# A four-layer graph network on one core: one square, one gate, 24 pieces and 100 products moved

## The reference, cut to what matters

```python
z = xx @ W_fc.T
e = sigmoid(concat([z[src], z[dst]]) @ W_attn.T)
w = exp(e - segment_max(e, dst)[dst])
h = segment_sum(w / segment_sum(w, dst)[dst] * z[src], dst)
K = mlp3(segment_sum((h @ W_encK.T + b_encK)[src], dst), K_...)
U = mlp3((h @ W_p1.T + b_p1)[src] + (h @ W_p2.T + b_p2)[dst], U_...)   # tanh, relu, linear
H = sum(segment_sum(K[src] * U, dst))
return grad(H) @ J.T - grad(H) @ D.T
```

## Time and profile before

| | us |
|---|---|
| three runs, median (lowest, highest) | 9449.99 (9428.79, 9453.63) |
| the profiled execution | 9455.71 |
| its span | 9453.9 |
| mean granted TensorE clock | 0.689 of 2.4 GHz |
| busy: PE, DVE, ACT, POOL | 4884.9, 4608.6, 2818.8, 5441.5 |
| A2 fetches (first, last) | 5605.5, 6935.1 |
| network, first spread scan on DVE | 6033.8 |
| weighing ahead | 7088.0 to 7504.8 |
| join of the network's ends (DVE) | 7607.1 |
| first operation of the last scan | 8147.6 |
| gradient products begin | 8414.5 |
| last weighing, PE | 8497.2 to 9125.7 |

### The profile page before, as it was taken

How to read it: one execution, slowest core, us unless ns; L and a number is a source line. 1 busy time by engine, 2 the same in 40 slices (tenths; PEclk the granted TensorE clock), 3 DMA queues, 4 the chain that set the end, 5 groups by cost and what they waited for, 6 DMA issues and landing times.

```text
span 9453.9 us, 77287 instructions
## 1 busy us (share of the span) xinstructions
PE 4884.9 (52%) x27914; PEld 2630.0 (28%) x27914; DVE 4608.6 (49%) x6100; ACT 2818.8 (30%) x2192; POOL 5441.5 (58%) x5420
## 2 busy tenths in 40 slices
PE   1000007999457777775577756344430035038976
PEld 0000006888113233231222222244430023032333
DVE  5789746777000000000398950488875410428870
ACT  0111110000000000000298940366657500429850
POOL 4777777777777777777610027688877777320000
PEclk6555555555578988987798975667665568559986
DMA  8887216444598989999799999455559848538767
GB/s 188 307 299 236 53 52 138 148 148 153 207 414 358 414 361 377 399 362 415 267 285 268 283 219 365 139 201 203 201 212 373 308 151 340 183 84 285 262 223 291
DMA packets 1203136, 2404.24 MB, mean 254 GB/s; under 512 B 566439, under 2 KB 818794, under 8 KB 1171354
## 3 DMA queue, kind: packets, MB, share of 16 engines
q1 hardware_dynamic: 996986, 2076.35, 61.8%
q0 software_dynamic: 187136, 170.29, 6.9%
q10 hardware_dynamic: 18720, 153.79, 4.2%
HBM read 1606.44 MB, written 711.62 MB: 245 GB/s over the span
## 4 chain that ended last, share of the span: by engine, by line
POOL 37%; DMA 26%; issue 12%; PE 11%; ACT 7%; ACTq 4%; DVE 2%; SPq 1%; DVEq 1%; POOLq 0%
POOL arena L486 18%; DMA arena<-cells_w 14%; POOL xd L489 9%; POOL cells_w L489 9%; DMA arena<-cells_c 8%; PE ps L699 5%; ACT arena L1031 3%; ACTq L1030 3%; ACT arena L1029 2%; PE ps L788 2%; DMA arena<-hot 1%; PE ps L880 1%; ACTq L2271 1%; PE ps L1162 1%; PE ps L1054 1%
## 5 line engine op out<-in xcount | busy, mean ns | idle before, releaser
L699 PE MATMUL ps<-arena 128*64 128x458 f32 (+2 forms) x7252 | 1345.0, 653 | 663.1 <-DMA arena<-cells_w 661.6
L486 POOL DMA_INDIRECT arena<-t_a,arena x832 | 947.9, 1139 | 1090.8 <-DMA t_a<-arena 837.7
L1054 PE MATMUL ps<-arena 128*33 128x400 f32 x6336 | 1173.1, 525 | 297.7 <-DVE arena L1049 289.8
L489 POOL DMA_INDIRECT sorted<-arena x832 | 843.8, 1014 | 289.9 <-issue 289.9
L489 POOL DMA_INDIRECT xd<-arena x832 | 832.0, 1000 | 260.9 <-issue 253.2
L717 DVE COPY carry<-ps 64x128 f32<-64x128 f32 (+1 forms) x5 | 1.5, 296 | 2006.1 <-PE ps L699 2006.1
L489 POOL DMA_INDIRECT cells_c<-arena x832 | 810.4, 974 | 293.5 <-issue 293.5
L486 POOL DMA_INDIRECT arena<-t_kv,idx x832 | 826.3, 993 | 258.7 <-issue 252.9
L489 POOL DMA_INDIRECT cells_w<-arena x832 | 813.7, 978 | 276.6 <-issue 276.6
L699 PEld LDWEIGHTS ps<-arena 128*64 128x64 f32 (+1 forms) x7252 | 425.5, 147 | 1579.0 <-issue 813.2
L1054 PEld LDWEIGHTS ps<-arena 128*33 128x33 f32 x6336 | 368.3, 115 | 1100.3 <-issue 662.9
(11 more groups left out here) (536 smaller groups left out, 9104.9 us busy)
## 6 DMA issues: line engine op xcount, KB each, us to landing
arena<-cells_w SPq DMA_DIRECT2D x245, 3200.0 KB
arena<-cells_c SPq DMA_DIRECT2D x294, 800.0 KB, 6.2
arena<-cells_turned SPq DMA_DIRECT2D x200, 800.0 KB, 8.2
cells_w<-arena SPq DMA_DIRECT2D x49, 3200.0 KB, 22.2
weighed_cells<-arena SPq DMA_DIRECT2D x68, 1600.0 KB, 14.2
arena<-weighed_cells SPq DMA_DIRECT2D x68, 1600.0 KB, 7.2
cells_c<-arena SPq DMA_DIRECT2D x50, 1600.0 KB, 5.8
cells_turned<-arena SPq DMA_DIRECT2D x100, 800.0 KB, 5.4
```

What stands on the lines that cost most here:

```text
L486: return pool.indirect_dma_start(dst, None, table, bass.IndirectOffsetOnAxis(ap=index, axis=0))
L489: return pool.indirect_dma_start(table, bass.IndirectOffsetOnAxis(ap=index, axis=0), source, None)
L699: mm = pe.matmul(bank[base + k][g * f:(g + 1) * f, 0:m], rows_of, tile[:, g * width + at:g * width + at + m], start=first, stop=last, skip ...
L1054: last = pe.matmul(bank[4 * h + c][64 * kind:64 * kind + 33, 0:400], own[:, t, :], moving[:, 400 * c:400 * c + 400], start=t == 0, stop=do ...
```

## The change

- `BEFORE` holds 23 row tiles instead of 17, so that 92 pieces are weighed ahead instead of 68, and the last weighing makes 108 instead of 132.
- `ahead_act` issues the tanh of the next piece between exp and square.
- In the network ACT squares tanh into UG2 at the end of `up_act`; DVE's pass for the slope goes. The signs move: the product is taken with (tanh^2 - 1), and PE's turned gates are copied with a scale of -1.
- The gates read the up products in PSUM instead of the relu's result in SBUF. They stand in `gate_step(k+1)`, between the copy and the scan of sums of step k. PE waits for gates as well as relu before it uses a PSUM bank again.
- `dhf` is split: the products of DFM1 and of the quarter sums are made once the quarters are there, ahead of `ends_pe("dsum")`, in banks 4 to 7; after `DD` only DFM2's 50 products are added.
- `XK_AT` 15 becomes 17, `GK_AT` 37 becomes 44, `HD_AT` 29 becomes 36.

```diff
-        BEFORE = range(0, NT, 3)
+        BEFORE = [t for t in range(NT) if t * 23 % NT < 23]
...
-        ALIAS_AT, XK_AT, GK_AT, HD_AT = 768, 15, 37, 29
+        ALIAS_AT, XK_AT, GK_AT, HD_AT = 768, 17, 44, 36
...
+        def gradient_pe(pe, source, weight, first):
+            if not first:
+                pe.wait_ge(S["fm_taken"], STEP["dhf"])
+            for t in range(NT):
+                to = bank[4 + t // 16][:, t % 16 * 32:t % 16 * 32 + 32]
...
+                last = pe.matmul(to, source[a, at:at + P], weight[a, :], start=first and t % 16 == 0, stop=not first,
+                                 skip_group_check=True)
+                if first:
+                    last = pe.matmul(to, SUMS3[0:96, t * P:t * P + P], fold[32][0:96, 0:32], start=False, stop=False,
+                                     skip_group_check=True)
...
+            tanh_act(0)
+            for i in range(len(todo)):
                 act.drain()
                 act.wait_ge(S["weighed"], base + max(0, 2 * i - 1))
-                act.activation(AHEAD_EXP, tanh, ACT.Exp, scale=0.5, bias=half[:]).then_inc(S["weights_made"], 1)
+                act.activation(AHEAD_EXP, AHEAD_TANH[i % 2], ACT.Exp, scale=0.5, bias=half[:]).then_inc(S["weights_made"], 1)
+                if i + 1 < len(todo):
+                    tanh_act(i + 1)
                 act.wait_ge(S["weighed"], base + 2 * i)
-                act.activation(AHEAD_SQUARE, tanh, ACT.Square).then_inc(S["weights_made"], 1)
+                act.activation(AHEAD_SQUARE, AHEAD_TANH[i % 2], ACT.Square).then_inc(S["weights_made"], 1)
...
+            def gate_step(k):
                 for u in range(UG):
                     t = slice(8 * u, 8 * u + 8)
                     dve.wait_ge(S["umlp_relu"], UG * k + u + 1)
-                    dve.scalar_tensor_tensor(hb[:, t, :], turned(UM[b], 64)[:, t, :], 0.0, turned(UXP[b], 64)[:, t, :], ALU.is_gt,
-                                             ALU.mult).then_inc(S["umlp_slope"], 1)
-                dve.drain()
+                    dve.scalar_tensor_tensor(rows(UHB, 64)[:, t, :], psO[u % 2].rearrange("p (j f) -> p j f", f=64), 0.0,
+                                             turned(UXP[k % 2], 64)[:, t, :], ALU.is_gt, ALU.mult).then_inc(S["umlp_slope"], 1)
+            spread_step(0)
+            gate_step(0)
             for k in range(2 * IT):
-                dve.wait_ge(S["umlp_tanh"], UG * (k + 1))
-                dve.scalar_tensor_tensor(slope, rows(UT, 64), -1.0, rows(UT, 64), ALU.mult, ALU.mult)
...
                 dve.tensor_copy(turned(UM[b], 64, 64), dr)
+                if k + 1 < 2 * IT:
+                    gate_step(k + 1)
                 dve.drain()
                 scan(dve, MASKS[b], UM[b], P, carry, wide=16, goes_on=firsts[b][:]).then_inc(S["scanned"], 1)
...
+                act.activation(UG2[k % 2], UT, ACT.Square)
...
-                    act.copy(packB[u % 2], psT[u % 2]).then_inc(S["umlp_turned_copied"], 1)
+                    act.activation(packB[u % 2], psT[u % 2], ACT.Copy, scale=-1.0).then_inc(S["umlp_turned_copied"], 1)
...
                         pe.wait_ge(S["umlp_relu"], UG * k + v - 1)
+                        pe.wait_ge(S["umlp_slope"], UG * k + v - 1)
...
+            await_made(pe, "dh_made")
+            gradient_pe(pe, DFM1, WD1, True)
             ends_pe(pe, "dsum", OD, 64, bank[3])
             await_made(pe, "dd_made")
             to_features_pe(pe, "DD", nodes(DD, 64), 4)
-            await_made(pe, "dh_made")
-            to_nodes_pe(pe, "dhf", DFM1, 64, 32, lambda c: WD1[64 * c:64 * c + 64, :], bank,
-                        more=((DFM2, 64, lambda c: WD2[64 * c:64 * c + 64, :]), (SUMS3, 96, lambda c: fold[32][0:96, 0:32])))
+            gradient_pe(pe, DFM2, WD2, False)
```

More of the change, by code:

```diff
@@ L1094, in ahead_act, with tanh_act @@
             base = 4 * NS
-            for i, j, phase, t, h in ahead():
+            todo = list(ahead())
+            def tanh_act(i):
+                _, j, phase, t, h = todo[i]
                 if j % len(BEFORE) == 0 and h == 0:
                     act.wait_ge(S[f"other{phase}"], 16 * 2)
-                tanh = AHEAD_TANH[i % 2]
-                act.activation(tanh, piece_of(AHEAD_OTHER[phase], h), ACT.Tanh, bias=a_dst[:, t:t + 1])
+                act.activation(AHEAD_TANH[i % 2], piece_of(AHEAD_OTHER[phase], h), ACT.Tanh, bias=a_dst[:, t:t + 1])
+            tanh_act(0)
+            for i in range(len(todo)):
                 act.drain()
                 act.wait_ge(S["weighed"], base + max(0, 2 * i - 1))
-                act.activation(AHEAD_EXP, tanh, ACT.Exp, scale=0.5, bias=half[:]).then_inc(S["weights_made"], 1)
+                act.activation(AHEAD_EXP, AHEAD_TANH[i % 2], ACT.Exp, scale=0.5, bias=half[:]).then_inc(S["weights_made"], 1)
+                if i + 1 < len(todo):
+                    tanh_act(i + 1)
                 act.wait_ge(S["weighed"], base + 2 * i)
-                act.activation(AHEAD_SQUARE, tanh, ACT.Square).then_inc(S["weights_made"], 1)
+                act.activation(AHEAD_SQUARE, AHEAD_TANH[i % 2], ACT.Square).then_inc(S["weights_made"], 1)
         def ahead_dve(dve):
@@ L1971, in _ @@
                     dve.wait_ge(S["umlp_relu"], UG * k + u + 1)
-                    dve.scalar_tensor_tensor(hb[:, t, :], turned(UM[b], 64)[:, t, :], 0.0, turned(UXP[b], 64)[:, t, :], ALU.is_gt,
-                                             ALU.mult).then_inc(S["umlp_slope"], 1)
-                dve.drain()
+                    dve.scalar_tensor_tensor(rows(UHB, 64)[:, t, :], psO[u % 2].rearrange("p (j f) -> p j f", f=64), 0.0,
+                                             turned(UXP[k % 2], 64)[:, t, :], ALU.is_gt, ALU.mult).then_inc(S["umlp_slope"], 1)
+            spread_step(0)
+            gate_step(0)
+            for k in range(2 * IT):
+                b = k % 2
+                slope, dr = rows(UG2[b], 64), rows(UDR[b], 64)
                 if k + 1 < 2 * IT:
@@ L1981, in _ @@
                         dve.wait_ge(S[f"d_kept{b}"], CREDIT + 16 * (k // 2))
-                    last = dve.scalar_tensor_tensor(dr[:, t, :], slope[:, t, :], 1.0, DTURN[u % 2].rearrange("p (j f) -> p j f", f=64),
+                    last = dve.scalar_tensor_tensor(dr[:, t, :], slope[:, t, :], -1.0, DTURN[u % 2].rearrange("p (j f) -> p j f", f=64),
                                                     ALU.add, ALU.mult)
@@ L2064, in _ @@
             dhf = nodes(DHF, 32)
-            for made, t, got in node_banks("dhf", 32, bank):
+            for made, t, got in node_banks("dhf", 32, bank[4:8]):
                 dve.wait_ge(S["fm_made"], made)
```

8 lines of the change are left out of this document (added).

## The result

| | before | after |
|---|---|---|
| runs, median (lowest, highest) | 9449.13 (9428.79, 9453.63) | 9387.7 (9386.71, 9395.25) |
| span of the profiled execution | 9453.9 | 9385.6 |
| weighing ahead | 7088.0 to 7504.8 | 7170.2 to 7720.3 |
| join on DVE | 7607.1 | 7729.6 |
| first operation of the last scan | 8147.6 | 8157.5 |

The ratio is 0.9942, with a 95% interval of 0.9929 to 0.9954: faster by 61 us (0.6%), beside a forecast of 9393. The span loses 68.3 us. Read from the table (last weighing is taken from its first product on PE to its last): the last scan starts 9.9 later, from there to the last weighing are 293.0 us for 349.7 (-56.7), the weighing takes 605.2 for 628.5 (-23.3), and 1.8 come back behind it.

What follows compares the result with a forecast made beforehand. POOL was taken to end last through the network, the weighing ahead and the scatter that sets the last scan's start. Sum: 9455.7 + 14 - 51 - 20 = 9399, with the median 5.7 below, so 9393; range 9300 to 9450.

Steps and rivals of the forecast that it cites:

- The step: Edge network: a step grows from 39.1 to 42.5 us as DVE waits for relus; network ends 94 us later.
- Rival A: Edge network: the step doesn't grow, relus being covered or 3 us earlier; 9327 us in the profiled execution, chance 0.26.
- rival C: Edge network: PE's clock falls to 1.2 GHz in the relu chain, 3.6 us a step; 9489 us, chance 0.11.
- The square hidden: Edge network: ACT's new square, 1.9 us, fits in; even at its upper bound ACT ends under the scan of sums.
- POOL: POOL's A2 fetches: 22.2 us a chunk behind XK, over at 6797, 139 us earlier; scatter reaches chunk 36 at 7615.
- Weighing ahead: Loop ahead of the join: 24 more pieces, 6.13 then 5.2 us each, over at 7724, stores landed at 7734.
- Rival B: Both weighings: transfers don't speed up, last 21 pieces stay at 6.13 us; 9444 us, chance 0.13.
- To the last scan: From join to last scan: 68 and 357 us unchanged, scan starts at 8159 against 8147.6, +14 us.
- 2 us for mask and copy: Ahead of the last scan: 2 us added for mask and copy on ACT, which began before DVE earlier.
- Gradient: Gradient products on PE: 200 of 300 records, 0.256 us each, move into the last scan; -51 us.
- Last weighing: Last weighing: PE's 267 us a half becomes the bound for 286.7; -20 us, bounds -26 and +10.
- 3 less for late transfers: Last weighing: 3 us taken off the 13 and 10 us gained in its halves, giving -20 us.

Runs made afterwards that it cites:

- e5: The changed kernel with the gates back behind the scan of sums, reading the relu's result in SBUF; ACT still squares: 9356.5 us, ratio 0.9904.
- e2: The kernel before with the network's edits alone (ACT squares, gates from PSUM ahead of the scan of sums, XK_AT 17): 9435.1 us, ratio 0.9975.
- e4: The kernel before without DVE's slope pass: ACT squares and the signs move, gates stay in SBUF in their old place; 9425.8 us, ratio 0.9961.
- e1: The kernel before with the split of dhf alone: 9398.0 us, ratio 0.9934.
- e3: The kernel before with 23 tiles weighed ahead for 17, HD_AT 29 and GK_AT 37 as before: 9509.3 us, ratio 1.0052.

## Experiments: what held the last scan

**e6_gk_earlier**: `GK_AT` 40 for 44.

> The changed kernel with GK_AT 40 for 44. In its trace DVE waited 93.3 us and PE 34.5 us for the one row of GK that POOL fetches at chunk 44 (7972.8), while the table was stored by about 7880, when POOL was at chunk 40. Theory: PE's 34 us go; the four quarters, 57 us each, end at about 8113 instead of 8149; POOL's own puts end at 8116 and are then the later of the two, so the last scan starts at about 8125 instead of 8157: 30 us faster than the changed kernel (about 9357). Rival (PE's wait is only moved, since the quarters' transfers need their time from the start): within 5 us of the changed kernel.

Measured: 9355.3, ratio 0.9906 (0.9891 to 0.9921), 33 us under the changed kernel. DVE's waits for the row of GK and for the last scan's first rows:

```profile
7889.04 0.18 DVE L845 CAST arena<-arena 128x32 bf16<-128x32 f32 x1 [13.71 <-DMA arena<-t_gk,alias_i]
...
8124.60 1.04 DVE L2074 COPY arena<-arena 128x1024 f32<-128x1024 f32 x1 [11.08 <-DMA arena<-xd]
```

The quarters end at 8113.0. POOL's last put is issued then too, and ACT loads the first rows behind it, at 8118.1: as expected, the puts are now the later of the two.

**e8_join_inside**: the join inside the loop.

```diff
+        PART_AHEAD = [region(a, QUARTER).bitcast(F16) for a in (6400, 8000, 28800)]
...
+            dve.wait_ge(S["crossed"], TURN["umlp"] + 1)
+            dve.tensor_copy(spread_carry[:, 0:P], bank[7][:, P:2 * P])
...
+                if i == 74:
+                    ends_dve(dve, "umlp", P, spread_carry)
...
-            ends_dve(dve, "umlp", P, bank[7][:, P:2 * P])
...
+            begin(dve, carry[:, 0:64], *DMASK)
             for q in range(4):
                 quarter_dve(dve, q)
```

`GK_AT` is 42, and ACT's first square of the loop waits for the first weights, so that the copy is out of the bank.

> The changed kernel with the join of the network's ends inside the loop of weighing ahead, ahead of piece 74 of 92 (the crossing sums copied out of PSUM first, the three input buffers of the loop moved off the region that the ends are fetched into), GK_AT 42, and the opening of the last scan issued ahead of the quarters so that its first rows are loaded early. Theory: POOL waited 137 us for this join; now it joins at about 7613, fetches the ends by 7680 beside the loop, and H is turned right behind the loop at about 7732 instead of 7798 (68 earlier); GK's row no longer stops PE (34 earlier); the 8 us for the last scan's first rows go: last scan at about 8048 instead of 8157, POOL's puts end at about 8000. About 9280, ratio to before 0.982. Rival (the last scan isn't reached by DVE's and PE's chain but by POOL's puts or by memory traffic, which stay): puts end near 8116 as now, 9350 or more.

Measured: 9290.7, ratio 0.9838 (0.9825 to 0.9852), 97 us under the changed kernel. POOL waits 32 us for the join, DVE 11 us for the row of GK, and between the last quarter and the last scan no idle time is left. Three edits act here together; only the row of GK was also run alone (33 us in e6):

```profile
7619.49 0.97 POOL L490 DMA_INDIRECT runs<-joined,join_s  x1 [32.06 <-DVEq L658]
```

```profile
7829.76 0.18 DVE L846 CAST arena<-arena 128x32 bf16<-128x32 f32 x1 [11.02 <-DMA arena<-t_gk,alias_i]
...
8052.03 2.01 DVE L960 COPY arena<-ps 96x400 f32<-96x400 f32 x4 [57.38 <-PE ps L891]
8054.18 1.03 DVE L2077 COPY arena<-arena 128x1024 f32<-128x1024 f32 x1
```

**e12_square_early**: e5 with the square moved.

```diff
                     act.activation(piece, piece, ACT.Tanh).then_inc(S["umlp_tanh"], 1)
+                act.drain()
+                act.activation(UG2[k % 2], UT, ACT.Square)
```

> The kernel e5 (changed kernel, gates back in SBUF behind the scan of sums) with ACT's square right behind the four tanh, in the 3.9 us that ACT there waits for PE's first turn, instead of behind the relus. Theory (with the gates in their old place ACT's own chain closes the step: tanh, turns, relus, square, source copy, mask; DVE waited 95 us for the mask): the square leaves the chain, a step takes 37.9 us instead of 39.8, the network ends about 48 us earlier (first piece at about 7066 instead of 7113), the wait for the mask falls under 60 us, and the loop of 92 pieces would end at about 7630; but POOL reaches chunk 36 only at 7677, so the join moves only from 7693 to about 7680: about 13 us faster than e5 (about 9343). Rival (the wait for the mask has another cause, the sums' scan or the source rows' transfer): step stays at 39.8, time as e5.

Measured: 9348.4, ratio 0.9895 (0.988 to 0.991), 8 us under e5, where 13 were expected; the intervals overlap, so it can't be told from none. The join came at 7676.3. The step fell by 0.9 us to 38.9, half of what I expected. In the 900 us from 6100 on, DVE's wait for the mask fell from 95 to 72 us, and ACT's wait for the A2 rows' transfer ahead of its source copy rose from 1.7 to 20.3:

```profile
ACT arena L2227 <- DMA arena<-a_edges: 20.3, 17, 3.6
```

**e11_tiles20**: e8 with 20 tiles, the join ahead of piece 71, `GK_AT` 41.

> The kernel e8 (join inside the loop) with 20 tiles weighed ahead for 23, the join ahead of piece 71 of 80, GK_AT 41. Theory: DVE's chain set the last scan in e8 (8054, POOL's puts done at 8012 with 32 us of waiting in them); 12 pieces of 6.07 fewer start the turn of H 66 to 73 us earlier; POOL's puts end at about 7982 and become the later: last scan at about 7990, 64 us earlier, for 12 more pieces in the last weighing, which cost 10 to 15 us (21 us for 24 pieces). About 50 us faster than e8, 9240. So beyond the join, more tiles weighed ahead cost more than they give. Rival (the count of pieces ahead isn't on the path any more): 10 us slower than e8.

Measured: 9235.7, ratio 0.9774 (0.9759 to 0.9789), 55 us under e8. POOL's last put is issued at 7998.6 and the last scan starts at 8010.6, waiting for it. That is 44 earlier than in e8, not the 64 expected:

```profile
7996.61 2.01 DVE L960 COPY arena<-ps 96x400 f32<-96x400 f32 x4 [55.26 <-PE ps L891]
8010.58 1.04 DVE L2077 COPY arena<-arena 128x1024 f32<-128x1024 f32 x1 [11.96 <-DMA arena<-xd]
```

I had put 10 to 15 us more on the last weighing. It took 596.7 us (8303.5 to 8900.2), 10 less than the 606.5 of e8. So the total came out near the 50 expected because two misses offset each other. The windows of this stage, e11 first, then e8:

```profile
8400.00:8600.00 200.00, 199.96 (x1194) 69.72 (x1190) 179.55 (x102) 190.12 (x125) 0.00 (x0) 1.00 0.97 337
```

```profile
8440.00:8640.00 200.00, 196.28 (x1168) 67.99 (x1166) 159.12 (x89) 167.51 (x109) 0.00 (x0) 1.00 1.00 355
```

With 20 tiles PE is 100% busy and the transfers have a share of 0.97; with 23 the share is 1.00 and PE at 98%. DVE's wait for rows of the counts (`arena<-cells_turned`) in the whole stage is 61.5 us in e11 and 126.3 in e8. With 23 the transfers have become the bound.

**e13_gates_between**: e8 with the square as in e12, `HD_AT` 35, `GK_AT` 40, the join ahead of piece 83, and

```diff
+                for i in range(8):
+                    piece = slice(16 * i * CJ, 16 * (i + 1) * CJ)
+                    dve.tensor_tensor_scan(UM[b][:, piece], MASKS[b], UM[b][:, piece], 0.0, ALU.mult, ALU.add)
+                    if i < UG and k + 1 < 2 * IT:
+                        gate(k + 1, i)
```

> The kernel e8 with 23 tiles, but the four gates, still read from PSUM, are put between the eight pieces of the scan of sums (one piece of 1.13 us ahead of each gate, where DVE waited 1.45 to 1.7 us for a relu), and the square behind the tanh; HD_AT 35, the join ahead of piece 83, GK_AT 40. Theory: of DVE's wait of 6.3 us a step for relus about 5 go, and the square's 1.9 us leave ACT's chain; the step takes 37.6 to 38.5 us instead of 41.8, the network ends 80 to 95 us earlier (first piece at about 7075), while POOL's fetches stay as quick (last at about 6790). The last scan is then set by POOL's puts at about 7985 instead of by DVE at 8054: about 9225, 65 us faster than e8. Rival (a step is bound by the chain of relus and PE's turns, not by DVE's order): step over 41, time as e8.

Measured: 9251.0, ratio 0.9791 (0.9778 to 0.9804), 40 us under e8, where 65 were expected. The step is 39.2 us and not 37.6 to 38.5 (ACT waited 27 us for A2 rows here too, and DVE 70 for the mask), so the first piece comes at 7098 for 7075 and the last scan at 8028.5 for 7985. POOL's fetches stay as quick as in the changed kernel (last at 6787.8). So the gates can read PSUM without the price of e2. DVE's gates in one step:

```profile
6529.20 1.22 DVE L2009 TENSOR_TENSOR_SCAN arena<-ps,arena 128x512 f32<-128x512 f32 x1
6530.37 1.04 DVE L1999 SCALAR_TENSOR_TENSOR arena<-ps,arena 128x512 f32<-128x512 f32 x1
6531.32 1.22 DVE L2009 TENSOR_TENSOR_SCAN arena<-ps,arena 128x512 f32<-128x512 f32 x1
6533.07 1.04 DVE L1999 SCALAR_TENSOR_TENSOR arena<-ps,arena 128x512 f32<-128x512 f32 x1 [0.53 <-ACT arena L2264]
```

**e14_all**: e13 with 22 tiles and the join ahead of piece 79.

> The kernel e13 with 22 tiles weighed ahead for 23 and the join ahead of piece 79 of 88 instead of 83 of 92. In e13 POOL waited 31.5 us for the join (it was there at 7578.7, DVE at 7610.2), its puts ended at 8021 and the last scan, for which DVE waited 23.5 us, started at 8028.5, while the quarters had ended at 8005. Theory (POOL's puts set the last scan in e13): DVE is at the join at about 7582, POOL's puts end at about 7993, the quarters at about 7985 to 8000, last scan at about 8003: 25 us earlier, less 4 us for the 4 pieces more in the last weighing: about 9230. Rival (with POOL and DVE that close, the first rows' load and the transfers take the time back): within 8 us of e13, 9245 to 9255.

Measured: 9234.0, ratio 0.9771 (0.9758 to 0.9784), 17 us under e13. DVE at the join and at the last scan:

```profile
7582.00 0.29 DVE L657 TENSOR_TENSOR joined<-joined,spread_carry 128x128 f32<-128x128 f32 x1 [1.53 <-DMA joined<-runs,join_s]
...
7972.54 2.01 DVE L960 COPY arena<-ps 96x400 f32<-96x400 f32 x4 [55.94 <-PE ps L891]
8001.27 1.05 DVE L2087 COPY arena<-arena 128x1024 f32<-128x1024 f32 x1 [26.72 <-DMA arena<-xd]
```

The last scan starts 27 us earlier, as the theory has it. The quarters are over at 7974.6; POOL's puts (last one at 7994.4) are what is left, in e11 as here. The last scan starts 9 us earlier than in e11, but the last weighing, with 22 tiles, takes 607.6 us, 11 more than there, so the total is that of e11. The quicker network with 20 tiles was not run. Both beat the kernel before by 2.3% and the changed one by 1.7%.

## Why the prediction was right, point by point

- **The step.** Forecast 42.5, measured 41.8, with the waits it named: each gate for its relu, the spread scan 0.8 us for the mask. The last relu ended at S+30.6 (forecast S+30.5), a gate took 1.03 (forecast 1.1). Weighing ahead began 82 us later, forecast 94: the 25 steps grew by 71 us together for the 85 forecast. Rival A (step of 39) is false. So is rival C: PE's granted clock over the network was 0.71, for 0.69 in the earlier trace rows, and a product of the relu chain took 1.16 us, as in the earlier trace rows.
- **The square hidden.** True in the changed order, with 2.5 us to spare. That it costs nothing is no property of ACT's idle time: in the old order (e4) the same 1.9 us lay on the path.
- **POOL.** Forecast last fetch 6797, measured 6786.2, longest 2.6 us. Two chunks ahead of XK gave 40 us (e4 against e5), forecast 41; a chunk behind XK is at 21.8 us ((6787 - 6023.6)/35), forecast 22.2. POOL waited 137 us at the join, forecast 110. The Trainium skill ("SBUF — State Buffer", "Who interferes with whom") has a DVE instruction with two SBUF inputs contend with GpSimd's reads, but saw a tensor_tensor not stall GpSimd's transfers. The first agrees with the trace, the second does not: from 6100 to 6800 us of the changed kernel, fetches that lie beside the four adds of `spread_step` (tensor_tensor, both inputs in SBUF) take 1.36 us in the mean and up to 1.70, for 0.94; and e5 and the changed kernel, which differ in the gates alone, are 78 us apart over the fetches.
- **Weighing ahead.** Forecast over at 7724, measured 7720.3; a piece took 5.98 us over all, and near 5.4 once POOL stood still, for the 5.2 of the estimate. That estimate took 395 GB/s from a stretch of other transfers; here, from 7600 to 7715 us, the engines moved 378 GB/s at a share of 1.05, and 2.05 MB at that rate are 5.4 us. Join forecast 7734, measured 7729.6, set by the loop as said. Rival B is false. The 358 GB/s of the Trainium skill ("DMA: Bandwidth & Descriptors", "Specifications") are passed by the 377 of the window here.
- **To the last scan.** Forecast +14, measured +9.9. 68 us to the first turn of H held. The 357 from there to the quarters' end came out at 351. One term was wrong: 2 us for mask and copy, where DVE waited 8.1 for the first rows of XD. By the program ACT loads them only once DVE has opened the scan, which stands right behind the last quarter; it issued them at 8149.6, POOL's puts being over at 8117. In e8 the scan is opened earlier, and the wait is gone. I took the 357 us as one block; e6 shows that about a tenth of it was a row fetched four chunks too late.
- **Gradient.** Forecast -51, with bounds of -45 and -52; measured -56.7, outside them. The 100 products took 18.65 us for the 26 forecast. The price of 0.256 us was the mean of 300, of which only the first 12 had a granted clock of 1.00; from 8416.3 on it was 0.50, 1.2 GHz, at 0.25 us each. Of the 100 that are left, 36 lie in the first 4.5 us at 0.90 (0.125 us each), and those at 0.50 take 0.21. So 3 to 4.5 of the 7 us are the clock (36 times 0.21 or 0.25 less 0.125); why a product at the same clock takes 0.21 for 0.25 is not shown.
- **Last weighing.** Forecast -20, measured -23.3. PE is 97 and 98% busy in the windows (99 was named as the sign), and in the second phase the transfers moved 353 GB/s with a share of 1.00. The "3 less for late transfers" was probably too small a term: with 20 tiles (e11) the same stage takes 9 us less than with 23.

The sum was right because its parts were, each within 6 us. How near it came is in part luck: the three parts all came out better than forecast, by 4, 6 and 3 us, and of these 13, 2 are lost behind the last weighing. That puts the profiled execution at 9387.6 for 9399, but in the changed kernel the median lies level with it, not 5.7 below, and so the forecast of 9393 misses by only 5. The sum's first part, the start of the last scan, was also a trade whose sides I did not price separately. e1, e2 and e3 show it: the gradient split carries the result; POOL's 149 us, the lengthened network and the 24 more pieces cancel each other to within the measurement (ratio 0.9934 of e1 alone, 0.9942 of the whole), and by the traces to -13 us (+9.9 at the last scan, -23.3 in the last weighing).

## What to carry to other kernels

When an engine gets ahead by 149 us, look for the place where it next waits for another engine, here a join that stood behind a whole loop in another engine's program, and move that join to the time at which the first engine arrives; this, with a row fetched and a scan opened in time, gave 97 us, more than the change itself (33 of them come from the row, by e6; the other two edits were not run apart). Take apart every interval that you carry over as a block: one row, fetched at a hand-set chunk number, held PE for 34 us in it. And an order in which an engine waits piece by piece for another (four gates, 1.6 us each) has room for its next independent work, piece by piece.

## What the runs showed that was not expected

- POOL's indirect fetches slow down beside some of DVE's passes in SBUF, and each of the two that were moved has its price: 33 us over 26 steps for the slope, 78 for the gates, with single fetches of up to 5.3 us (e5), while with the gates' main operand in PSUM the longest took 2.62 (e2). The 78 are not an effect of the longer step: in e13, at 39.2 us a step, the fetches take 1183.5 us (5604.3 to 6787.8), 73 less than in e5. The fetches from 6100 to 6800 us, each put down to the DVE pass that it overlaps longest, say which passes cost: 99 beside the gates from PSUM took 0.94 us in the mean (longest 0.97), as beside the scans; 34 beside the gates from SBUF 2.76 (e5, longest 5.26), 31 beside the slope 1.84 (before), and those beside the copy of DVE from SBUF to SBUF still 2.31 in the changed kernel.
- More work done ahead does not always shorten the stage that it is done for. My sum had the last weighing falling with every tile; it was shortest at 20 (times in us; the waits are those of the whole stage):

| tiles weighed ahead | last weighing | PE waits for DVE's pieces | DVE waits for rows of the counts |
|---|---|---|---|
| 17 (before) | 628.5 | 52.5 | 24.4 |
| 20 (e11) | 596.7 | 29.8 | 61.5 |
| 22 (e14) | 607.6 | 38.3 | 111.2 |
| 23 (after; e8) | 605.2; 606.5 | 34.0; 36.8 | 122.8; 126.3 |

With 17, PE waits for DVE's pieces, of which ACT makes its part at 98% busy; with 22 or 23 the transfers' share is at 0.97 to 1.00 and the pieces come late because the rows of the counts do.
